# Attention and top-1 expert block on one core: gate logits computed as extra columns of the value and output products, VectorE's order in a slot, and the place of the expert loads

## Reference, cut to what matters

```python
h = _layernorm(x, axis=-1) * (1 + cb) + sb
# _mha(h): qkv = h @ Wqkv.T + bqkv; softmax over the 16 rows of one position; o @ Wo.T + bo
y = _layer_norm(h + _mha(h, Wqkv, bqkv, Wo, bo), g1, be1)
# _moe(y): logits = y @ Wg.T; idx = argmax(logits)
#          out = relu(y @ W1[idx] + b1[idx]) @ W2[idx] + b2[idx]
z = _layer_norm(y + _moe(y, Wg, W1, b1, W2, b2), g2, be2)
x = x + gb * z
```

## Time and profile before

| what | value |
|---|---|
| the profiled execution's own time | 1225.19 us |
| its span | 1223.0 us |
| busy: TensorE, VectorE, ScalarE, GpSimd | 90%, 79%, 75%, 70% |
| mean granted TensorE clock | 0.942 |
| first stage | up to about 802 us |
| slots of the second stage | about 802 to 1041 us |
| first load of sorted rows | 1047.28 us |
| expert products | from 1055 us to the end |

### The profile page before, as it was taken

One profiled execution on the slowest core, in us unless ns is written; L12 is line 12 of the kernel. 1 busy time (PEld: TensorE's weight loads), 2 busy tenths in 40 slices (PEclk: granted clock), 3 DMA queues, 4 the chain that ended last, 5 costly groups with the idle time before them and its releaser, 6 DMA issues. The chain is left out here.

```text
span 1223.0 us, 49591 instructions
## 1 busy us (share of the span) xinstructions
PE 1102.8 (90%) x17489; PEld 902.1 (74%) x17489; DVE 971.2 (79%) x4190; ACT 921.4 (75%) x3404; POOL 854.5 (70%) x685
## 2 busy tenths in 40 slices
PE   4899999999999999999999999947999984599992
PEld 2688888888888888888888887725787773488882
DVE  6898998898898898988989987546788764188884
ACT  2689989989889899899899898836776752366661
POOL 2777877877877878777878776554576677067775
PEclk9899999999999999999999999969988885699996
DMA  6766666766666666667667667352243123676110
GB/s 197 208 166 167 177 169 164 182 166 168 175 167 170 177 167 170 176 156 183 166 170 175 163 156 188 96 184 80 62 137 103 55 81 135 172 196 178 58 37 22
DMA packets 111026, 180.88 MB, mean 148 GB/s; under 512 B 19726, under 2 KB 64177, under 8 KB 110656
## 3 DMA queue, kind: packets, MB, share of 16 engines
q1 hardware_dynamic: 102944, 158.53, 50.3%
q0 software_dynamic: 6400, 16.82, 3.8%
q10 hardware_dynamic: 1440, 2.36, 0.8%
HBM read 35.20 MB, written 24.73 MB: 49 GB/s over the span
## 5 line engine op out<-in xcount | busy, mean ns | idle before, releaser
L612 POOL TENSOR_TENSOR qk<-mm,sw 128x1024 f32<-128x1024 f32 x128 | 305.0, 2383 | 96.2 <-DMA sw<-mm 96.1
L685 ACT ACTIVATE pr<-sm,mn 128x96 f32<-128x96 f32 x1024 | 368.6, 371 | 0.0
L618 POOL TENSOR_TENSOR pr<-pr,ri 128x768 f32<-128x768 f32 x128 | 189.1, 1478 | 73.0 <-DVE ri L540 72.9
L501 DVE TENSOR_TENSOR mm<-bank,cos 128x512 f32<-128x512 f32 x256 | 175.3, 685 | 69.9 <-PE bank L324 58.8
L685 ACT ACTIVATION_READ_ACCUMULATOR pr<-sm,mn 128x1 f32 x1024 | 202.2, 197 | 0.0
L513 DVE CUSTOM_DVE_ANT_0 sm<-bank,msk 128x96 f32<-128x96 f32 x1024 | 190.9, 252 | 3.4 <-PE bank L350 3.4
L502 DVE TENSOR_TENSOR mm<-bank,sin 128x512 f32<-128x512 f32 x256 | 174.0, 680 | 0.0
L377 PE MATMUL bank<-pT,vw 96*64 96x64 f32 x4096 | 147.5, 225 | 0.0
L377 PEld LDWEIGHTS bank<-pT,vw 96*64 96x64 f32 x4096 | 129.8, 138 | 17.1 <-issue 5.8
L676 ACT ACTIVATE pT<-bank 96x512 f32<-96x512 f32 x256 | 137.4, 588 | 0.5 <-PE bank L392 0.5
L392 PE MATMUL bank<-ident,pr 128*96 128x128 f32 x1024 | 133.6, 274 | 0.0
(11 more groups left out here) (206 smaller groups left out, 2492.8 us busy)
## 6 DMA issues: line engine op xcount, KB each, us to landing
sw<-mm SPq DMA_DIRECT2D x512, 128.0 KB, 2.4
vw<-vn SPq DMA_DIRECT2D x128, 192.0 KB, 2.6
vw<-vn SPq DMA_DIRECT2D x128, 128.0 KB, 2.3
rr<-sorted_scratch SPq DMA_DIRECT2D x72, 192.5 KB, 2.8
vw<-vn SPq DMA_DIRECT2D x96, 64.0 KB, 2.2
xt<-in_x SPq DMA_DIRECT2D x16, 256.0 KB, 3.9
x_scratch<-x SPq DMA_DIRECT2D x16, 256.0 KB, 2.5
rr<-x_scratch SPq DMA_DIRECT2D x16, 256.0 KB, 3.1
```

The costliest lines, as they stand in the source:

```text
L501: dve.tensor_tensor(mm[s % 2][:, 0, j, :], PJ[u % 2][:, :], cos[:, :], ALU.mult)
L612: pool.tensor_tensor(qk[i % 2][:, :, 32:], mm[i % 2][:, 0, :, :], sw[i % 2][:, :, :], ALU.add)\
L618: pool.tensor_tensor(t, t, ri[i % 2][:, :].unsqueeze(2).to_broadcast([P, 8, WK]), ALU.mult)\
L685: ins = act.activation(pr[i % 2][:, h, p, :], ms_[i % 2][:, h, p, :], ACT.Exp, scale=-1.0, bias=mn[i % 2][:, h, p:p + 1], accum_out=sums[i ...
```

## The change

The value weights get 8 further columns (`wve`, 136 wide), which hold the gate weights times g1, less their mean; the output weights get 8 (`woe`), which hold the output weights times those columns. The value product so gives the logits' share of `h2`, which ScalarE copies into 8 new columns of `h2`; the output product gives that of the attention, and the residual sum `uu`, now 136 wide, holds the logits but for the scale of the row and a constant. VectorE multiplies by the scale of the norm chain of the same slot and adds the constant (`lgb`). The transposes t3, the copy `yT` and the product lg are gone.

Beside this:

- `hT` is copied without interchange, and `oT` is interchanged instead. The biases of query, key and output are corrected for bo (`fbn`).
- "v" and "wo" take two adjacent banks each. A table of positions replaces the plain turn through the ring.
- Argmax moves from `u = s - 5` to `u = s - 4`, rk, addresses and scatters from `u = s - 6` to `u = s - 5`; on TensorE rk stands behind v. `LAST` is one less.
- VectorE takes the maximum and difference of the scores ahead of the residual sum and its statistics.
- The load of `w1s` stands behind the query copy of one slot later; the bias product stands ahead of wo, in its banks, and the addition to `b1t` ahead of the residual sum.
- The one-time work `prepare()` moves to the head of VectorE's program, and a new `gate()` makes the new weights, with a few products and copies on TensorE and ScalarE.

```diff
-banks = [top.enter_context(nc.psum_tensor(f"bank{i}", [P, 512], F32)) for i in range(8)]
+banks = [top.enter_context(nc.psum_tensor(f"bank{i}", [P, 512], F32)) for i in range(4)]
+wide = [top.enter_context(nc.psum_tensor(f"bank{4 + 2 * i}", [P, 1024], F32)) for i in range(2)]
+banks += [wide[i // 2][:, 512 * (i % 2):512 * (i % 2) + 512] for i in range(4)]
...
 s_sl = sem("s_sl")
 X, RING = banks[0:4], banks[4:8]
-FIRST, LAST = -3, NQ + 6
-
-order = []
+FIRST, LAST = -3, NQ + 5
+
+r_use, r_pos, last_use, r_prev, pos = {}, {}, {}, {}, 0
 for s in range(FIRST, LAST):
-    order += [w for w in (("t1", s), ("q", s), ("k", s), ("rk", s - 6), ("pt", s - 2), ("v", s), ("t3", s - 5),
-                          ("lg", s - 5), ("wo", s - 3)) if 0 <= w[1] < NQ]
-r_use = {w: n for n, w in enumerate(order)}
-emptied = {"t1": s_he, "q": s_qe, "k": s_ke, "pt": s_pe, "v": s_ve, "t3": s_ye, "lg": s_le, "wo": s_u, "rk": s_rkd}
+    for kind, u in (("t1", s), ("q", s), ("k", s), ("pt", s - 2), ("v", s), ("rk", s - 5), ("wo", s - 3)):
+        if 0 <= u < NQ:
+            size = 2 if kind in ("v", "wo") else 1
+            pos += pos % size if kind != "rk" else 1 - pos % 2
+            held = [(pos + n) % 4 for n in range(size)]
+            r_use[kind, u], r_pos[kind, u] = len(r_use), pos % 4
+            r_prev[kind, u] = {last_use[n] for n in held if n in last_use}
+            last_use.update({n: (kind, u) for n in held})
+            pos += size
+emptied = {"t1": s_he, "q": s_qe, "k": s_ke, "pt": s_pe, "v": s_ve, "wo": s_u, "rk": s_rkd}
 
 def ring(*w):
-    return RING[r_use[w] % 4]
+    return RING[r_pos[w]]
+
+def pair(*w):
+    return wide[r_pos[w] // 2][:, :].rearrange("p (a b) -> p a b", a=2)
+
+def blocks(*w):
+    return pair(*w)[:, :, 0:2 * CE].rearrange("p a (g c) -> p a g c", c=CE)
+
+def halves(t):
+    return t.rearrange("p (a g) c -> p a g c", a=2)
 
 def quad(v):
...
+    pool.wait_ge(s_le, 2 * (s - 6) + 1)
 pool.tensor_scalar(r, m[:, :, :, 1], EPS, None, ALU.add).then_inc(s_ln, 1)
 pool.tensor_scalar(z, m[:, :, :, 0], -1.0, None, ALU.mult).then_inc(s_ln, 1)
...
 def _(pe):
     def bank(*w):
-        n = r_use[w]
-        if n >= 4:
-            kind, v = order[n - 4]
+        for kind, v in sorted(r_prev[w]):
             pe.wait_ge(emptied[kind], v + 1)
-        return RING[n % 4]
+        return ring(*w)
...
+pe.transpose(X[1][:, 0:P], wfo, ident[:, :]).then_inc(s_eo, 1)
 pe.wait_ge(s_ao, 1)
+pe.matmul(X[2][:, 0:NE], gcol[:, 0:1].to_broadcast([P, P]), wg, start=True, stop=True)
+pe.matmul(X[2][:, NE:2 * NE], gcol[:, 1:2].to_broadcast([P, P]), wg, start=True, stop=True)
+for k in range(3):
+    ins = pe.matmul(X[2][:, 2 * NE + k:2 * NE + k + 1], wf[:, k * C:(k + 1) * C], gcol[:, 2:3], start=True, stop=True)
+ins.then_inc(s_eo, 1)
+pe.wait_ge(s_do, 13)
+pe.matmul(X[3][:, 0:NE], woT[:, :], wve[:, C:], start=True, stop=True).then_inc(s_eo, 1)
...
+if quad(u):
+    bank("v", u)
+    dst = blocks("v", u)
+    for g in range(4):
+        ins = pe.matmul(dst[:, g // 2, g % 2, :], hT[u % 2][:, g * P:(g + 1) * P], wve[:, :],
+                        start=True, stop=True)
+    ins.then_inc(s_r, 1)
+u = s - 5
 if quad(u):
     pe.wait_ge(s_oh, u + 1)
     dst = bank("rk", u)
...
-    dst = bank("v", u)
-    for g in range(4):
-        ins = pe.matmul(dst[:, g * C:(g + 1) * C], hT[u % 2][:, g * P:(g + 1) * P], wf[:, 2 * C:],
-                        start=True, stop=True)
-    ins.then_inc(s_r, 1)
-u = s - 5
-if quad(u):
-    pe.wait_ge(s_cy, u + 1)
-    dst = bank("t3", u)
-    for j in range(4):
-        ins = pe.transpose(dst[:, j * P:(j + 1) * P], quad_rows(u)[:, j, 0:C], ident[:, :])
     ins.then_inc(s_r, 1)
 u = s - 2
 if quad(u):
...
     ins.then_inc(s_pv, 1)
-u = s - 5
-if quad(u):
-    pe.wait_ge(s_ye, u + 1)
-    dst = bank("lg", u)
+u = s - 3
+if quad(u):
+    pe.wait_ge(s_oe, 4 * u + 4)
+    bank("wo", u)
+    dst = blocks("wo", u)
+    e = u - 2
+    if 0 <= e < NE:
+        pe.wait_ge(s_ws[e % 2], 16 * (e // 2 + 1))
+        for c in range(4):
+            pe.matmul(pair("wo", u)[:, 0, 2 * CE + c:2 * CE + c + 1], w1s[e % 2][:, c * P:(c + 1) * P],
+                      gcol[:, 1:2], start=True, stop=True)
     for j in range(4):
-        ins = pe.matmul(dst[:, j * NE:(j + 1) * NE], yT[:, j * P:(j + 1) * P], wg, start=True, stop=True)
-    if u < NE:
-        pe.wait_ge(s_ws[u % 2], 16 * (u // 2 + 1))
-        for c in range(4):
-            ins = pe.matmul(dst[:, 4 * NE + c:4 * NE + c + 1], w1s[u % 2][:, c * P:(c + 1) * P],
-                            gcol[:, 1:2], start=True, stop=True)
-    ins.then_inc(s_r, 1)
-u = s - 3
-if quad(u):
-    pe.wait_ge(s_oe, 4 * u + 4)
-    dst = bank("wo", u)
-    for j in range(4):
-        ins = pe.matmul(dst[:, j * C:(j + 1) * C], oT[u % 2][:, j * P:(j + 1) * P], wfo,
+        ins = pe.matmul(dst[:, j // 2, j % 2, :], oT[u % 2][:, j * P:(j + 1) * P], woe[:, :],
                         start=True, stop=True)
...
 for s in range(FIRST, LAST):
-    e = s - 4
-    if 2 <= e < NE:
-        act.wait_ge(s_wlo, e - 1)
-        act.wait_ge(s_bx, e - 1)
...
         act.wait_ge(s_sc, u - 1)
-    act.activation(qT[u % 2][:, :], ring("q", u)[:, :], ACT.Identity, bias=fb[:, 0:1]).then_inc(s_qe, 1)
+    act.activation(qT[u % 2][:, :], ring("q", u)[:, :], ACT.Identity, bias=fbn[:, 0:1]).then_inc(s_qe, 1)
+e = s - 5
+if 2 <= e < NE:
+    act.wait_ge(s_wlo, e - 1)
+    act.wait_ge(s_r, r_use["wo", e] + 1)
+    act.dma_start(w1s[e % 2][:, :], a["W1"][:, e * DF:(e + 1) * DF]).then_inc(s_ws[e % 2], 16)
...
-    act.activation(va[u % 3][:, :, :], ring("v", u)[:, :].rearrange("p (g c) -> p g c", g=4), ACT.Copy)\
-        .then_inc(s_ve, 1)
-u = s - 5
-if quad(u):
-    act.wait_ge(s_r, r_use[("t3", u)] + 1)
-    if u >= 1:
-        act.wait_ge(s_r, r_use[("lg", u - 1)] + 1)
-    act.activation(yT[:, :], ring("t3", u)[:, :], ACT.Identity, scale=gcol[:, 0:1], bias=gcol[:, 1:2])\
-        .then_inc(s_ye, 1)
+    act.activation(halves(va[u % 3][:, :, :]), blocks("v", u)[:, :, :, 0:C], ACT.Copy)
+    act.activation(halves(h2[u % 7][:, :, C:]), blocks("v", u)[:, :, :, C:], ACT.Copy).then_inc(s_ve, 1)
 u = s + 2
 if quad(u):
...
 for j in range(4):
-    act.activation(oT[u % 2][:, j * P:(j + 1) * P], X[j][:, 0:P], ACT.Identity, bias=fb[:, 2:3])\
+    act.activation(oT[u % 2][:, :].rearrange("c (g j k) -> c j g k", g=4, j=4)[:, j],
+                   X[j][:, 0:P].rearrange("c (g k) -> c g k", g=4), ACT.Identity, bias=fbn[:, 2:3])\
         .then_inc(s_oe, 1)
...
+    dve.tensor_copy(lgb[:, :], X[2][:, NE:2 * NE]).then_inc(s_do, 1)
+    dve.tensor_tensor(fbn[:, :], fb, X[2][:, 2 * NE:2 * NE + 3], ALU.add).then_inc(s_do, 1)
+    dve.wait_ge(s_do, 12)
+    dve.scalar_tensor_tensor(out=wve[:, C:], in0=X[2][:, 0:NE], scalar=-1.0 / C, in1=wgs[:, :],
+                             op0=ALU.mult, op1=ALU.add).then_inc(s_do, 1)
+    dve.wait_ge(s_eo, 3)
+    dve.tensor_copy(woe[:, C:], X[3][:, 0:NE]).then_inc(s_do, 1)
 
 dve.wait_ge(s_po, 3)
+prepare()
 for s in range(FIRST, LAST):
     if s == FIRST + 1:
-        prepare()
-    u = s - 4
-    if quad(u):
-        dve.wait_ge(s_r, r_use[("wo", u)] + 1)
-        dve.wait_ge(s_h2, 2 * u + 2)
-        if u >= 2:
-            dve.wait_ge(s_cy, u - 1)
-        dve.tensor_tensor(uu[u % 2][:, :, :], ring("wo", u)[:, :].rearrange("p (j c) -> p j c", j=4),
-                          h2[u % 7][:, :, :], ALU.add).then_inc(s_u, 1)
-        dve.wait_ge(s_u, u + 1)
-        if u >= 2:
-            dve.wait_ge(s_ln, norms(s - 2))
-        stats(uu[u % 2], 1, u, mv[s % 2], s_b2)
+        gate()
     u = s - 1
     if quad(u):
...
                           ALU.subtract).then_inc(s_dd, 1)
+u = s - 4
+if quad(u):
+    dve.wait_ge(s_r, r_use[("wo", u)] + 1)
+    dve.wait_ge(s_h2, 2 * u + 2)
+    if u >= 2:
+        dve.wait_ge(s_cy, u - 1)
+    e = u - 2
+    if 0 <= e < NE:
+        dve.tensor_tensor(b1t[:, 4 * e:4 * e + 4], b1t[:, 4 * e:4 * e + 4],
+                          pair("wo", u)[:, 0, 2 * CE:2 * CE + 4], ALU.add).then_inc(s_bx, 1)
+    dve.tensor_tensor(halves(uu[u % 2][:, :, :]), blocks("wo", u), halves(h2[u % 7][:, :, :]), ALU.add)\
+        .then_inc(s_u, 1)
+    dve.wait_ge(s_u, u + 1)
+    if u >= 2:
+        dve.wait_ge(s_ln, norms(s - 2))
+    stats(uu[u % 2][:, :, 0:C], 1, u, mv[s % 2], s_b2)
 u = s + 1
 if quad(u):
-    v = h2[u % 7][:, :, :]
...
-u = s - 5
-if quad(u):
-    dve.wait_ge(s_r, r_use[("lg", u)] + 1)
+u = s - 4
+if quad(u):
+    dve.wait_ge(s_ln, norms(s))
     if u >= 1:
         dve.wait_ge(s_oh, u)
-    if u < NE:
-        dve.tensor_tensor(b1t[:, 4 * u:4 * u + 4], b1t[:, 4 * u:4 * u + 4],
-                          ring("lg", u)[:, 4 * NE:4 * NE + 4], ALU.add).then_inc(s_bx, 1)
-    dve.tensor_copy(lg[:, :, :], ring("lg", u)[:, 0:4 * NE].rearrange("p (j e) -> p j e", j=4))\
+    dve.tensor_tensor(lg[:, :, :], uu[u % 2][:, :, C:], rs[s % 2][:, 1, :].unsqueeze(2).to_broadcast([P, 4, NE]),
+                      ALU.mult).then_inc(s_le, 1)
```

(3 more changed lines are left out.)

69 lines of the change are left out of this document (39 added, 30 removed).

## The result

The changed kernel takes 1250.87 us (median of 4 runs, 1248.47 to 1251.86) against 1225.22 of the kernel before, a ratio of 1.0214 (95% interval 1.0193 to 1.0236). That is clear of no change, though the interval reaches to both sides of 2%. The forecast of 1217 and its range are missed on the wrong side. The profiled execution took 1250.5 us, span 1248.5.

A forecast was written before the change was run, and what follows sets the result against it. TensorE, with stops and a low clock, was taken to bound slots 4 to 15, GpSimd the drain. Terms -3.1 (slots), -2.9 (drain) and nothing (start) made -6.0: 1219.2 from 1225.2 profiled, forecast 1217 us against the median, range 1206 to 1229.

The forecast's parts named there:

- The saving of 1.35 us: TensorE, each slot: t3 and lg go, v and wo grow slightly, net 1.35 us less work.
- The short cycle: Slots from 4 on: scores, VectorE's maximum, difference and sum, then key product; TensorE idles 1.6 us, cycle 10.5 us.
- so the wait is covered: VectorE's logits wait for the same slot's norm chain: some 3.2 us, covered unless GpSimd is over 1.8 us late.
- Losses before: TensorE, slots 4 to 15: stops and clock lose 28.4 us before, 24.4 after, of which 17.1 stay unhidden.
- the forecast of 144.9: Slots 4 to 15: undisturbed 127.8 us plus 17.1 of losses, -3.1 us against 148.0.
- the bound of 156: Slots 4 to 15: upper bound with nothing hidden and no loss smaller, +8 us.
- Drain -2.9: Slot 16's scores to the last scatter, bound by GpSimd: 43.4 us instead of 46.3.
- Start: nothing: Start of VectorE's program, prepare() and gate(): costed at nothing; uncovered under 3 us once.
- The slower case, idle time that costs the clock: TensorE behind the scores: idle 1.6 us a slot lowers the clock to half the time at 1.2 GHz; 1232, chance 0.15.
- The port lock: VectorE's two new logit operations blocked by GpSimd: 1.0 us a slot, +6 net, 1229; chance 0.06.
- The late expert load: Ahead of wo: w1s landing above 4.8 us stops TensorE in six slots, up to 1 us each; +3, 1220; chance 0.08.
- I am wrong if slots without a stop take over 11.5: The prediction's own mark: slots where nothing stops take 10.5 to 11 us; wrong above 11.5 or under 10.2.

The follow-up runs named there:

- run 5: Changed kernel with another bank table: transposes, query, key and ranks avoid the pair holding the last output product; VectorE's order as changed; 1240.74 us, ratio 1.013.
- run 2: Changed kernel with ScalarE's output copy put ahead of the normalization hc; 1241.48 us, ratio 1.0137 to the kernel before.
- run 1: Changed kernel with VectorE's residual sum and statistics back ahead of maximum and difference of the scores; 1225.27 us, ratio 1.0029 to the kernel before.
- run 3: Kernel before with only VectorE's order changed: maximum and difference of the scores ahead of residual sum and statistics; 1238.72 us, ratio 1.0131.
- the useless product: An unread 128x512 product between query and key product per slot: 1227.69 us in the kernel before, 1249.81 in the changed one, 1225.27 in the best combination.
- the best combination: Changed kernel with sum ahead of maximum, output copy ahead of normalization, run 5's banks and 64 small products once ahead of stage two; 1218.07 us, ratio 0.9981.
- the sum-first kernel: The kernel of run 1: changed kernel with the residual sum ahead of the maximum on VectorE; 1225.27 us, with 64 products ahead 1222.68.
- the shift: 64 products of 8 columns once ahead of TensorE's stage two, moving all its later code back; in the changed kernel 1242.63 us, ratio 1.0179.
- run 6: One unread 128x512 product between query and key product of each slot: changed kernel 1249.81 us (ratio 1.0227), kernel before 1227.69 (1.0052).
- run 4: Kernel before with only the load of the next expert's weights moved behind the query copy on ScalarE; 1222.17 us, ratio 1.0006.
- run 7: 64 products of 8 columns once ahead of TensorE's stage two: sum-first kernel 1222.68 us, kernel before 1228.06, changed kernel 1242.63.

## Why the prediction was wrong

- *"Before, TensorE alone needed 10.2. The saving of 1.35 us is eaten by the serial piece of VectorE."* The short cycle was there: the wait was foretold at 1.6 us and measured 1.15, in 11 slots of 12. Cutting it alone returned 10.1 us (run 5).
- ***"Between the statistics and the logits VectorE has some 5 us of other work ... so the wait is covered."*** This is the step that failed. It asked only who waits for the norm chain on VectorE, and there the logits indeed waited just once, for 0.4 us. The chain's other reader is ScalarE's `hc`, which waited for it 6 times, 9.1 us, with the output copy queued behind it, and the mask products behind that. The prediction put this path at nothing. It takes 11.8 us from scores to scores where the short cycle has 10.5, TensorE waited 6.3 us at its end, and cutting it alone returned 9.4 us (run 2). Run 1 shows that the order, which makes both cycles, is the whole loss.
- *"Losses before: 10.6 of stops and 17.8 of clock ... After: 4% less code and more idle time for its fetch, 10 ... 14.4. Of these 24.4 I hide ..."* This term failed too, and it is the larger part in size. Before, the stops were 11.7. After, they were 15.9, and a clock of 0.82 is 36% of 170.4 us at the low clock, which loses 30.7 where before it lost 17.8: 46.6 in place of 24.4. The slots came 25.5 us above the forecast of 144.9. Of this 6.3 is the wait for `foT`; the other 19.2 are losses, as 170.4 less 127.8 and 6.3 leaves 36.3 where the forecast had 17.1 (an estimate: the undisturbed 127.8 is kept, which slots 7, 9 and 13 come near to). It is above even the bound of 156, which assumed that no loss would grow. The order has a share in the clock as well, since run 1 has 0.87 with nothing else changed and run 3, with the old work, 0.86 for 0.88; how much of the loss is the clock's and how much the waits' stays open. The premise that less code gives fewer stops does not hold: run 1, with the code of the changed kernel, has 21.3. Nor do more idle time or more work give fewer in every kernel: the useless product went with 3.9 for 11.7 before the change, but 18.9 for 15.9 in the changed kernel and 22.2 for 16.6 in the best combination.
- *Drain -2.9.* Right in mechanism and near in size: norm chain of slot 16 at 3.8 us behind the last scores (forecast 3.8), 8.8 to the next (9.3), 13.5 for the last part (13.7), 42.6 in all (43.4). Mask and scores of slot 16 took 1.6 us longer than before, 0.9 of it a stop, so -2.1 remained to the end of the span.
- *Start: nothing.* The operations of `gate()` cost nothing seen, but slots 0 to 3 took 4.3 us more. The kernel before with 64 products ahead shows the same (36.5), the sum-first kernel with them 31.7. So the code's place, which the forecast did not count, can make such a difference; in the changed kernel itself the shift took back 2.1 of the 4.3, and the rest is open.
- *The rivals.* The slower case, idle time that costs the clock, named the right sign. It took half of the time at the low clock and put the point where it decides at a third; 36% came. What the clock cost beside the cycles is not parted from them: run 6 raised it by 0.04 for no gain in time, slot 11 had 2.08 us for 1.13 on its path. Its 1232 would not have held the result either. The port lock came too (means of 439 and 581 ns for the two logit operations against 192) and no price of it is seen, as VectorE still waited 33.3 us for scores. The late expert load did not come: no wait for `w1s` stands among TensorE's waits, and run 4 has no price for the moved load in the kernel before. *"I am wrong if slots without a stop take over 11.5"*: they took 10.7 to 11.4, so even that mark would not have warned of a loss of 22 us.

## What to carry to other kernels

When a step is moved later on an in-order engine, follow every reader of what it produces, once around the loop on each engine, and add what stands in the queue ahead of the next hand-over; here the second reader of one norm chain closed a cycle that the first did not show. Before pricing removed work at its length, ask what the engine would do in its place: a useless product of the same size, added, is a cheap test, if it is compared with as much code without the work. Here it cost about half of its length. Differences below 4 to 8 us between versions of this kernel should be measured at more than one shift of the code.

## What the runs showed of the hardware

- TensorE's stops go with the arrival of its code. By narrow windows on the instruction queue q8 in run 1, packets start at 851.9, 871.8, 880.15, 898.8, 907.65 and 935.55, and stops end at 854.29, 874.44, 882.85, 901.35, 910.13 and 937.98, 2.4 to 2.7 us on each time. The longest stops are those where the packet starts late: that of 910.13 began at 907.0, its packet at 907.65, and none had started since 898.8. Why it was not fetched ahead stays open. Most packets are followed by no stop.
- 64 products of 32x32, 1.3 to 1.9 us of work, are 128 product records and as many weight loads, 256 instructions. With the blocks of 256 that fit the places in run 7, every such burst crosses a boundary; a stop stands in only some of them.
- The same work, placed 128 instructions further on, differs by 8.2 us of 1250 by the times and 4.3 by the ratios, and in slots 0 to 3 alone by 4.5 of 32 (kernel before) and 5.4 of 37 (sum first). The clock of slots 4 to 15 differs too: 0.91 for 0.88 in the kernel before, 0.87 for 0.82 in the changed one.
- Two tiny products a slot changed the clock of slots 4 to 15 from 0.88 to 0.94 in the one profile that there is of each, with the stops all but the same (10.3 and 11.7). The shift alone, with no product in the slots, went with 0.91. No run here explains it.
